# Path blocks of 12 and 12 edge tiles instead of 14 and 10, with six tiles of the last block summed by TensorE, and one scatter ahead of the last block

## The reference, cut to what matters

```
x = x + L0_gnn(layernorm(x));  x = x + L0_ffn(layernorm(x))
# L1_gnn: 16 segments of 32 numbers per row, 64 paths (i1, i2, i3) with a coefficient each
x1 = xn[src]                     # 4352 x 16 x 32, gathered rows
x2 = edge_attr                   # 4352 x 16 x 32
contrib  = coef[p] * x1[:, i1[p], :] * x2[:, i2[p], :]      # for each of 64 paths
edge_out = zeros.at[:, i3, :].add(contrib)                  # sum of the paths by output segment
x = x + zeros(256, 512).at[dst].add(edge_out)               # scatter of the edges to the nodes
x = x + L1_ffn(layernorm(x))     # 16 experts, a controller, f1 and f2
```

## Time and profile before

| | us |
|---|---|
| median of 3 runs | 276.57 (276.3 to 276.63) |
| the profiled execution | 278.61 |
| its span in the trace | 276.8 |
| busy: TensorE, its weight loads | 264.2, 185.3 |
| busy: VectorE, ScalarE, GpSimd | 223.9, 166.9, 39.5 |

### The profile page before, as it was taken

The page is one execution under the profiler, slowest core; times in us unless marked ns, Lnnn a source line. Parts: engine busy times, 40 slices in busy tenths (PEclk is TensorE's granted clock), DMA queues, the critical chain, the costliest instruction groups (busy, mean ns, idle before and its releaser), DMA issues.

```text
span 276.8 us, 5669 instructions
## 1 busy us (share of the span) xinstructions
PE 264.2 (95%) x1639; PEld 185.3 (67%) x1639; DVE 223.9 (81%) x662; ACT 166.9 (60%) x341; POOL 39.5 (14%) x52
## 2 busy tenths in 40 slices
PE   6999999999998889999999999969999999999996
PEld 4666788886443779996678787755666664468633
DVE  5977664299657979999999999999999997755372
ACT  6921431011427479978887878399889829353260
POOL 4000150060007736662000000000000000000000
PEclk9999999999999999999999999988999999999999
DMA  6699990000014735656233000004444429000002
GB/s 208 222 409 410 437 404 17 0 4 1 36 39 117 197 111 149 163 155 182 76 107 125 2 0 2 2 19 153 155 152 153 150 81 344 36 2 2 2 0 76
DMA packets 12592, 33.91 MB, mean 123 GB/s; under 512 B 3345, under 2 KB 3602, under 8 KB 12306
## 3 DMA queue, kind: packets, MB, share of 16 engines
q1 hardware_dynamic: 10482, 26.73, 26.7%
q0 software_dynamic: 2080, 6.82, 8.8%
HBM read 32.50 MB, written 1.05 MB: 121 GB/s over the span
## 4 chain that ended last, share of the span: by engine, by line
PE 85%; DVE 6%; ACT 3%; issue 3%; DMA 1%; DVEq 1%; ACTq 1%; SPq 0%
PE psum L1345 15%; PE psum L1294 15%; PE psum L1248 10%; PE psum L1348 8%; PE psum L1272 5%; PE psum L1277 4%; PE psum L1300 3%; PE psum L1419 3%; PE psum L1445 3%; PE psum L1191 3%; PE psum L1177 2%; PE psum L1336 2%; PE psum L1131 2%; DVE big L1039 2%; PE psum L1229 1%
## 5 line engine op out<-in xcount | busy, mean ns | idle before, releaser
L605 ACT ACTIVATE prod<-edges,coef_b 128x320 f32 (+1 forms) x78 | 43.2, 591 | 16.0 <-PE psum L1348 8.1
L1294 PE MATMUL psum<-big,dst_oh 128*128 128x512 f32 x108 | 50.6, 593 | 0.2 <-DVE big L1039 0.2
L1345 PE MATMUL psum<-prod,ident 128*128 128x128 f32 x160 | 31.8, 292 | 0.8 <-DVE prod L1029 0.7
L1029 DVE TENSOR_TENSOR prod<-big,prod 128x320 f32<-128x320 f32 (+1 forms) x53 | 29.2, 552 | 2.7 <-ACT prod L605 1.7
L1345 PEld LDWEIGHTS psum<-prod,ident 128*128 128x128 f32 x160 | 24.5, 190 | 10.3 <-issue 9.5
L1294 PEld LDWEIGHTS psum<-big,dst_oh 128*128 128x128 f32 x108 | 18.7, 191 | 14.7 <-issue 14.3
L1248 PE MATMUL psum<-edges,big 128*128 128x256 f32 x128 | 28.3, 380 | 0.0
L1248 PEld LDWEIGHTS psum<-edges,big 128*128 128x128 f32 x128 | 24.1, 190 | 3.5 <-issue 0.3
L1039 DVE TENSOR_TENSOR big<-big,prod 128x64 f32 (+2 forms) x80 | 26.3, 329 | 0.0
L605 ACT ACTIVATE xparts<-edges,coef_b 128x320 f32 (+1 forms) x48 | 25.7, 586 | 0.8 <-PE psum L1345 0.8
L470 POOL DMA_INDIRECT big<-xn_rows,big x16 | 16.9, 1054 | 33.0 <-DMA xn_rows<-xn 23.5
(11 more groups left out here) (223 smaller groups left out, 530.6 us busy)
## 6 DMA issues: line engine op xcount, KB each, us to landing
big<-in_w SPq DMA_DIRECT2D x3, 2048.0 KB, 16.4
edges<-in_edge SPq DMA_DIRECT2D x1, 3584.0 KB, 24.1
edges<-in_f SPq DMA_DIRECT2D x7, 512.0 KB, 3.4
edges<-in_edge SPq DMA_DIRECT2D x1, 2560.0 KB, 23.8
edges<-in_edge SPq DMA_DIRECT2D x5, 512.0 KB, 3.6
edges<-in_f SPq DMA_DIRECT2D x1, 2560.0 KB, 10.0
big<-in_f SPq DMA_DIRECT2D x4, 512.0 KB, 3.5
big<-in_gnn_w SPq DMA_DIRECT2D x1, 1024.0 KB, 6.0
```

The source lines that it names most:

```text
L605: nc.scalar.activation(slot(n)[:, 0:BLOCKS[b], :], segment(edges_of(b), single_column(words, p)), ACT.Copy, scale=coef_b[:, p:p + 1]).then ...
L1029: nc.vector.tensor_tensor(v, segment(xg[:, 0:tiles, :], first_column(words[b], p)), v, ALU.mult).then_inc(mults, 1)
L1294: last = mm(bank[2 + h], dst_oh[:, n % DR, h * P:(h + 1) * P], tile_sums(b, t), start=False, stop=False)
L1345: last = mm(path_sums(to), ident[:], product[:, 0:PT].rearrange("p t u -> p (t u)"), start=False, stop=True, skip_group_check=True)
```

## The change

The blocks become 10, 12 and 12 tiles, and TensorE keeps 8, 6 and 6 of them, so that VectorE sums 2, 6 and 6 tiles where it summed 2, 8 and 6. Block 2 now has the second matmul per path and the extra zero matmul, and it uses six PSUM banks. The first scatter of block 1's tiles is made before block 2's banks are cleared (`EARLY`); the other eleven lie among block 2's paths. In the tail there are four whole scatters and eight split ones (three and seven before). With smaller slots the ring has 13 of them. Block 2's rest sums move to the room of block 0's edge rows and are cleared by one GpSimd instruction once block 0's products are done, in place of ScalarE's six writes and their wait. Block 2's edge rows get a region of their own with 12 tiles and are loaded in six DMAs. f1 and f2 lie partly in the room of block 0's sums, and the f1 loads wait for the tenth scatter besides.

```
--- before.py
+++ after.py
@@ -35,9 +35,10 @@
     GR = 32 // TG
     NR = P // 32
 
-    BLOCKS = [10, 14, 10]
-    FIRST = [0, 10, 24]
-    KEPT = [8, 6, 4]
+    BLOCKS = [10, 12, 12]
+    FIRST = [0, 10, 22]
+    KEPT = [8, 6, 6]
+    EARLY = [0, 0, 1]
     PT = 4
     PE_TILES = 8
     PT2 = [k - PT for k in KEPT]
@@ -49,14 +50,14 @@
     QT = -(-PE_TILES // 4)
     BMAX = max(BLOCKS)
     LATE = FIRST[2]
-    SLOTS = 12
-    OWN_SLOTS, XN_SLOTS, PART_SLOTS = 5, 2, 3
+    SLOTS = 13
+    OWN_SLOTS, XN_SLOTS, PART_SLOTS = 5, 2, 4
     DR = 5
     BEHIND = 14
     DIRECT = [0, 2, 0]
     SUMS_LEAD = 8
     FREE_SLOTS = 2
-    SPLIT = 7
+    SPLIT = 8
     KEPT_AT = BLOCKS[2] - KEPT[2] - (BLOCKS[2] - SPLIT)
     SPLIT_ROWS = 2
     OH_A, OH_B = 7, 9
@@ -111,7 +112,7 @@
         src_t = sb("src_t", [P, H, PE_TILES * P], BF16)
         xn_rows = nc.dram_tensor("xn_rows", [N, D], F32, kind="Internal").ap()
 
-        big = sb("big", [P, (2 * BLOCKS[0] + BLOCKS[1] + BLOCKS[1] - KEPT[1]) * D + T * STEP_W // 2 + 2 * T + 3 * NP])
+        big = sb("big", [P, (BLOCKS[2] + BLOCKS[1] + BLOCKS[1] - KEPT[1] + BLOCKS[0]) * D + T * STEP_W // 2 + 2 * T + 3 * NP])
         prod = sb("prod", [P, OWN_SLOTS, BMAX, U])
         dst_oh = sb("dst_oh", [P, DR, N])
         xparts = sb("xparts", [P, 3, H, D], BF16)
@@ -162,7 +163,8 @@
         w2_sb = take([HC, D])
         src_oh = take([T, N], BF16)
         take = carve(big[:, :])
-        x1g = [take([BLOCKS[0], D]), take([BLOCKS[1], D])]
+        late_edges = take([BLOCKS[2], D])
+        x1g = [late_edges[:, 0:BLOCKS[0], :], take([BLOCKS[1], D])]
         late_sums = take([BLOCKS[1] - KEPT[1], D])
         sum_room = [take([BLOCKS[0], D]), late_sums]
         step_room = take([T * STEP_W], BF16)
@@ -173,8 +175,8 @@
         path_i = take([NP, 3], I32)[0:1]
 
 
-        kept_sums = [sum_room[0][:, 0:KEPT[0], :], x1g[1][:, 0:KEPT[1], :], sum_room[0][:, 0:KEPT[2], :]]
-        rest_sums = [sum_room[0][:, KEPT[0]:, :], sum_room[1], sum_room[0][:, KEPT[2]:, :]]
+        kept_sums = [sum_room[0][:, 0:KEPT[0], :], x1g[1][:, 0:KEPT[1], :], late_edges[:, 0:KEPT[2], :]]
+        rest_sums = [sum_room[0][:, KEPT[0]:, :], sum_room[1], edges[:, 0:BLOCKS[2] - KEPT[2], :]]
         take = carve(x1g[1].rearrange("p t f -> p (t f)"))
         sum_parts = take([SPLIT, 3, D], BF16)
         late_rows = edges[:, LATE:T, :]
@@ -182,8 +184,7 @@
         rows_of = [x1g[0], x1g[1], late_rows]
 
         def edges_of(b):
-            lo = FIRST[b] if b < NB - 1 else 0
-            return edges[:, lo:lo + BLOCKS[b], :]
+            return edges[:, FIRST[b]:FIRST[b] + BLOCKS[b], :] if b < NB - 1 else late_edges
 
         take = carve(late)
         xnT = take([KC, N])
@@ -213,14 +214,15 @@
         route_bias = take([G + EX])
         tw_sb = take([H * EX])
         w_cat = take([KC, G + EX])
-        take = carve(x1g[0].rearrange("p t f -> p (t f)"))
+        take = carve(sum_room[0].rearrange("p t f -> p (t f)"))
         f1_parts = [take([KC // 2, f1.shape[1]])]
-        ctrl_sb = take([KC, ES])
+        f2_parts = [take([2, D])]
+        ctrl_sb = carve(edges[:, BLOCKS[2] - KEPT[2]:BLOCKS[0], :].rearrange("p t f -> p (t f)"))([KC, ES])
         take = carve(edges[:, BLOCKS[0]:LATE, :].rearrange("p t f -> p (t f)"))
         f1_parts.append(take([KC // 2, f1.shape[1]]))
-        f2_lo = take([6, D])
+        f2_parts.append(take([4, D]))
         f2_hi = carve(late)([FC - 6, D])
-        take = carve(big[:, BLOCKS[0] * D:])
+        take = carve(big[:, :])
         xnT2 = take([KC, N])
         logit = take([P])
         top = take([PH])
@@ -288,8 +290,8 @@
             return kept_sums[b][:, i, :] if i < KEPT[b] else rest_sums[b][:, i - KEPT[b], :]
 
         def scatter_paths(b):
-            n = BLOCKS[b - 1] if b else 0
-            return [1 + i * (NP - 4) // n for i in range(n)]
+            n = BLOCKS[b - 1] - EARLY[b] if b else 0
+            return [-1] * EARLY[b] + [1 + i * (NP - 4) // n for i in range(n)]
 
         scatter_tile = {n: t for b in range(NB) for n, t in scatter_order(b)}
         split_tiles = [t for _, t in scatter_order(NB - 1)][BLOCKS[NB - 1] - SPLIT:]
@@ -317,7 +319,7 @@
             return f1_parts[kc // 2][:, kc % 2, :]
 
         def f2_sb(c):
-            return f2_lo[:, c, :] if c < 6 else f2_hi[:, c - 6, :]
+            return f2_parts[0][:, c, :] if c < 2 else f2_parts[1][:, c - 2, :] if c < 6 else f2_hi[:, c - 6, :]
 
 
         x_in, idx_in, w_in, w1_in, w3_in, w2_in = (sem(n) for n in
@@ -414,13 +416,14 @@
             sp.wait_ge(mults, NP * (NB - 1))
             sp.dma_start(ctrl_sb, rows(ctrl)).then_inc(ctrl_in, 16)
             w = f1.shape[1] // 2
+            sp.wait_ge(scattered, FIRST[1])
             for i in range(2 * KC):
                 sp.wait_ge(mults, NP * (NB - 1) + 4 + 5 * i)
                 sp.dma_start(f1_sb(i // 2)[:, i % 2 * w:(i % 2 + 1) * w], rows(f1)[:, i // 2, i % 2 * w:(i % 2 + 1) * w])\
                     .then_inc(f1_in, 16)
             for i in range(0, 6, 2):
                 sp.wait_ge(mults, NP * (NB - 1) + 44 + 3 * i)
-                sp.dma_start(f2_lo[:, i:i + 2, :], rows(f2)[:, i:i + 2, :]).then_inc(f2_in, 16)
+                sp.dma_start(f2_parts[0] if i == 0 else f2_parts[1][:, i - 2:i, :], rows(f2)[:, i:i + 2, :]).then_inc(f2_in, 16)
             sp.wait_ge(mults, NP * NB)
             sp.dma_start(f2_hi, rows(f2)[:, 6:FC, :]).then_inc(f2b_in, 16)
             for i, (h, lo, hi) in enumerate(((0, 0, D), (1, 0, D // 2), (1, D // 2, D))):
@@ -492,6 +495,8 @@
             gather_rows(0)
             gather_rows(1)
             gather_rows(2)
+            pool.wait_ge(mults, NP)
+            nc.gpsimd.memset(rest_sums[2], 0.0).then_inc(cleared[2], 1)
 
         @block.scalar
         def _(act):
@@ -631,11 +636,6 @@
                 b, p = n // NP, n % NP
                 if b == 1 and p == SUMS_LEAD:
                     copy_sums(0, 0, 8)
-                if b == 2 and p == 0:
-                    act.wait_ge(scattered, FIRST[1])
-                    for i in range(BLOCKS[b] - KEPT[b]):
-                        nc.scalar.activation(rest_sums[b][:, i, :], zero_b[:, 0:1].broadcast_to([P, D]), ACT.Copy)\
-                            .then_inc(cleared[b], 1)
                 for m in range(DR, T - SPLIT):
                     if scattered_at(m - DR) + BEHIND == n:
                         one_hot(m)
@@ -1015,7 +1015,7 @@
                     else:
                         dve.wait_ge(row_in[b], 16 * tiles)
                     if direct(b, 0):
-                        dve.wait_ge(edge_in[b], 16)
+                        dve.wait_ge(edge_in[b], 16 if b < NB - 1 else 16 * (BLOCKS[b] // 2))
                 v = slot(n)[:, 0:tiles, :]
                 if direct(b, p):
                     if n >= SLOTS:
@@ -1032,7 +1032,7 @@
                 b, p = divmod(n, NP)
                 if p == 0:
                     dve.wait_ge(mults, n + 1)
-                    dve.wait_ge(cleared[b], (1, 2, BLOCKS[b] - KEPT[b])[b])
+                    dve.wait_ge(cleared[b], (1, 2, 1)[b])
                 if n:
                     dve.wait_ge(sums, n)
                 v = segment(rest_sums[b], out_column(words[b], p))
@@ -1329,6 +1329,8 @@
                 if b == 0:
                     pe.wait_ge(gathered, PE_TILES // 2)
                     pe.wait_ge(gathered_odd, PE_TILES // 2)
+                for n, t in scatters[:EARLY[b]]:
+                    scatter(b - 1, n, t)
                 for i, q in enumerate(sum_banks(b)):
                     if b:
                         pe.wait_ge(block_out, banks_before(b - 1) + i + 1)
```

More of the change, by code:

```diff
@@ L633, in _ @@
                     copy_sums(0, 0, 8)
[L634 to L638, removed]
                 for m in range(DR, T - SPLIT):
```

8 lines of the change are left out of this document (4 added, 4 removed).

## The result

The changed kernel takes 287.75 us (287.75 to 287.76, 4 runs) against 276.44 (276.30 to 276.63) for the kernel before: ratio 1.0409, 95% interval 1.0396 to 1.0422, 11.3 us slower. 289.4 was forecast, 286.6 to 291.8 as the range.

What follows compares the result with a forecast made beforehand. TensorE and VectorE were taken to run level in blocks 1 and 2, with TensorE full in block 2. Terms -2.9 + 2.0 + 10.7 + 3.0 = +12.8 on 276.57 gave 289.4 us, range 286.6 to 291.8.

Steps and rivals of the forecast that it cites:

- Block 1, -2.9: Block 1: TensorE's own rate limits the gain to 2.9 us, though VectorE needs 8.6 us less.
- Block 2, +10.7: Block 2: TensorE, with second and zero matmuls added and three scatters fewer, goes from 39.1 to 49.8 us, +10.7.
- The 0.6 for a slow clock: Start of block 2: 0.6 us for the rest of TensorE's slow clock after the border, within the +10.7.
- The first rival: Block 2: VectorE is the bound and TensorE has room; about -2.4, 274.2 us; chance 0.04.
- The border, +2.0: Between blocks 1 and 2: wait for copies and slow clearings make the border 6.8 us instead of 4.8, +2.0.
- The wait for banks 0 and 1: Border: TensorE stands 1.65 us because the copies of these banks stand behind the scaling of paths 6 to 10.
- The second rival: Border: the clock stays at 2.4 GHz; +11.4 in all, 288.0 us; chance 0.18.
- The third rival: Border costs more (late ScalarE, VectorE dry and low clock, or slow level twice as long): +1.5 to 2.5, 291.5; chance 0.10.
- the fourth: Border: the early scatter waits for VectorE's last sum of block 1, not filling the copy wait; +1.7, 291.1; chance 0.03.
- The tail, +3.0: Tail: one more whole scatter (1.72 us) and one more split tile (1.28) on TensorE, copies covered, +3.0.
- The offset of 2.04: Whole kernel: the median lay 2.04 us below the profiled execution, and the forecast kept that offset.

Runs made afterwards that it cites:

- Without the second matmul: The changed kernel with block 2's second matmul per path left out, zero matmul kept: 279.32 us, +2.8 against the kernel before.
- the clearing on GpSimd alone: The kernel before with the last block's rest sums cleared by one GpSimd instruction instead of ScalarE's six writes: 278.51 us against 278.78, ratio 0.9996.
- the kept tiles alone: The kernel before, blocks 10, 14, 10, with the last block's kept tiles raised from four to six and eight split tiles: 296.67 us, +17.9.
- the three variants: Changed kernel without block 2's second matmul (279.32 us) or with four kept tiles in the last block (287.88); kernel before with clearing on GpSimd (278.51).
- no zero matmuls, before: The kernel before without its 31 zero matmuls in block 1: 276.30 us against 276.32.
- early scatter put back: The changed kernel with the early scatter put back among block 2's paths (EARLY 0): 292.25 us, +13.5 against the kernel before.
- fewer adds, before: The kernel before with VectorE's adds cut by two tiles in blocks 1 and 2: 274.39 us against 276.32, ratio 0.9937.
- the block sizes alone: The changed kernel with four kept tiles in the last block instead of six and seven split tiles: 287.88 us, +9.1 against the kernel before.

## Why the prediction was right

**Block 1, -2.9, exact.** VectorE saved more than TensorE could follow, and TensorE's own rate (4.56 us for six paths and a scatter) set the end. Before the change 8.6 us less of VectorE's adds are worth 3.2 in the profiled execution (1.9 in the median); after it, 15.5 us less change the time by 0.03; the 31 zero matmuls are worth nothing before the change and 1.7 after it. That is shown from both sides.

**Block 2, +10.7 forecast, +10.3 measured.** The mechanism held: 32 pairs of 0.95 and 11 scatters give 49.2, measured 49.3. The 0.6 for a slow clock was not paid. Without the second matmul the time falls by 8.5 and VectorE sets the end. The first rival, that TensorE has room, is refuted: with TensorE's load share at 38.8 of 49.3 us its pitch does not yield, and taking 15.5 us from VectorE gives nothing. The Trainium skill ("Perfetto Trace Analysis", Identifying the Most-Contended Engine) has TensorE's headroom judged by MFU, the share of the peak rate that is used, and by the busy share of weight loads. Read by that share alone, 38.8 of 49.3 us, a fifth of TensorE would be free; the trace disagrees, since the pitch stayed at 0.95. One reading was off, without weight in the sum: I had TensorE full in block 2 of the kernel before. It was near it, but the clearing on GpSimd alone shows VectorE setting that end.

**The border, +2.0 forecast, +1.3 measured.** The step that was mis-sized is the clock: after a gap of 1.64 us it stayed at 2.4 GHz. The wait for banks 0 and 1 was there, and is worth 1.8 by itself. The second rival, 288.0, thus lay nearest to the time, and nearly all of the 1.5 us by which the change was forecast too large is this one term (1.4 over both stages). The third rival needed a low clock and falls with it; the fourth falls because the early scatter started right behind the last path (178.83). I had given the second 0.18 because the one gap of that length in the trace had cost the clock; one gap was too little to go by.

**The tail, +3.0 forecast, +2.8 measured.** TensorE ran it without a wait, with the copies under the whole scatters. I had counted two split tiles among the work that needs no copy; it is one, since the second one's parts come behind the copies in ScalarE's order. With four whole scatters ahead that made no difference; with two, in the kept tiles alone, TensorE stood 0.40 us.

**What cost nothing** did so: GpSimd's clearing took 2.66 us, and VectorE's period is 0.74 beside 0.735; the last layer takes 35.5 us in both, so f1 and f2 were in time. The offset of 2.04 between the profiled execution and the median was right to carry, but by luck: I did not know what it was. It is the stall in block 0, 2.3 us by the first scatter; the kernels profiled at 276.2 and 276.3 us have none.

**Where I was wrong behind it**: the 1 us that VectorE would gain from the moved clearing, and the zero matmuls at their full length. In the three variants where I had VectorE set the end of block 2 the forecast came out too fast by 0.8, 1.0 and 3.3 us, the last mostly by the clock.

## What to carry to other kernels

Where two engines run level, moving work from one to the other gains only what the second one's own rate lets through; read that rate where it runs unhindered (a burst behind a late start), and sum its instructions before crediting the first with anything. Price a short instruction by what the stream's pitch becomes with and without it, not by its length. And look where the receiving engine is fullest: here the tail and block 2 took 13 us of TensorE for 4.3 of VectorE (64 x 0.067, two tiles' adds).

## What the runs showed of the hardware

The length of TensorE's gap alone does not tell whether its clock falls. At the border of blocks 1 and 2, in single profiled executions, it fell after gaps of 1.69 (before) and 2.12 us (kept tiles alone), and stayed up after 1.64 (after), 1.64 (no zero matmuls, before), 2.38 (early scatter put back) and 3.13 us (fewer adds, before); the two longest:

```profile
186.03 0.39 PE L1338 MATMUL psum<-big,zero_b 128*128 128x512 bf16 x1 [2.38 <-ACT big L625]
```

```profile
182.14 0.39 PE L1337 MATMUL psum<-big,zero_b 128*128 128x512 bf16 x1 [3.13 <-ACT big L615]
```

The stall in block 0 says the same. Five profiled executions have it, with TensorE idle 0.4 to 1.1 us at a time between 95 and 99 us; the clock fell to 0.50 behind it in two (clearing on GpSimd alone, early scatter put back) and stayed at 1.00 in three. What decides stays open. The clock fell, too, where TensorE waited only 0.2 to 0.4 us at a time for VectorE over several paths, just ahead of the tail, and cost 1.9 and 3.1 us there (without the second matmul, and the block sizes alone). An engine that is starved a little at the end of a stage can cost more in the next than in its own.
